# One-core graph-attention kernel: layer 1 gets three places for h and attention values two tiles behind, beside the transposes

## The reference, cut to what matters

```
# layer 0 of the reference (the layer that the title calls layer 1)
h = x @ W                                  # 12 heads of 64 features
th = tanh(h)
attn = (th @ w_src) + (th @ w_dst)^T       # per head, 64 x 64 per graph
attn = leaky_relu(attn, 0.2);  attn = where(adj, attn, -999);  attn = softmax(attn)
feat = elu(attn @ h + b)
gate = sigmoid(x @ H_w.T + H_b)
x = layernorm(x + gate * feat + (1 - gate) * x)
# second layer: six-head attention under the mask adj, output product, layernorm
```

## Time and profile before

| what | value |
|---|---|
| median of 3 runs | 2755.78 us (2752.92 to 2757.6) |
| the profiled execution's own time | 2753.85 us |
| its span | 2752.1 us |
| PE busy | 2723.5 us (99%) |
| PEld busy | 2516.5 us (91%) |
| DVE busy | 1679.9 us (61%) |
| ACT busy | 1211.6 us (44%) |
| POOL busy | 926.7 us (34%) |
| chain that ended last | PE 88%, DVE 6%, DMA 2%, issue 2%, ACT 1% |

### The profile page before, as it was taken

The page is one execution under the profiler, slowest core; times in us unless marked ns, Lnnn a source line. Parts: engine busy times, 40 slices in busy tenths (PEclk is TensorE's granted clock), DMA queues, the critical chain, the costliest instruction groups (busy, mean ns, idle before and its releaser), DMA issues.

```text
span 2752.1 us, 51889 instructions
## 1 busy us (share of the span) xinstructions
PE 2723.5 (99%) x20988; PEld 2516.5 (91%) x20988; DVE 1679.9 (61%) x3335; ACT 1211.6 (44%) x3109; POOL 926.7 (34%) x566
## 2 busy tenths in 40 slices
PE   8999999999999989999999999999999999999998
PEld 7777878888878889999999999999999999999998
DVE  7899998888888664444445444444545444444543
ACT  5666676666666633323332333323333333233332
POOL 2353334443444123323333233323332333323330
PEclk9999999999999999999999999999999999999999
DMA  6655665555555521222222222222222222222220
GB/s 183 172 138 145 168 161 135 145 138 141 143 137 138 169 75 58 82 70 81 59 69 71 82 70 58 81 79 73 59 71 72 79 70 63 77 82 70 59 70 24
DMA packets 306895, 269.50 MB, mean 98 GB/s; under 512 B 227808, under 2 KB 244192, under 8 KB 306656
## 3 DMA queue, kind: packets, MB, share of 16 engines
q1 hardware_dynamic: 306656, 266.19, 35.3%
HBM read 142.65 MB, written 75.89 MB: 79 GB/s over the span
## 4 chain that ended last, share of the span: by engine, by line
PE 88%; DVE 6%; DMA 2%; issue 2%; ACT 1%; POOL 0%; SPq 0%; DVEq 0%; ACTq 0%; POOLq 0%
PE ps_hg L1057 22%; PE ps_k L70 15%; PE ps_a L1232 15%; PE ps_a L70 14%; PE ps_q L70 14%; PE ps_s L1173 2%; PE ps_c L1198 2%; PE ps_pv L1089 1%; DMA dst_all<-dst_scratch 1%; PE ps_t L1076 1%; PE ps_pt L1198 1%; ACT logits L563 1%; DMA dst_scratch<-dst 1%; PE ps_pt L1180 1%; DVE logits L787 1%
## 5 line engine op out<-in xcount | busy, mean ns | idle before, releaser
L1057 PE MATMUL ps_hg<-w_hi,xT 128*128 128x512 f32 x2268 | 745.3, 401 | 3.0 <-DVE h_one L820 2.7
L1057 PEld LDWEIGHTS ps_hg<-w_hi,xT 128*128 128x128 f32 x2268 | 426.2, 188 | 106.2 <-issue 4.8
L1057 PE MATMUL ps_hg<-w_lo,xT 128*128 128x512 f32 x1134 | 448.5, 395 | 0.0
L70 PE MATMUL ps_k<-x1T_hi,wk_hi 128*128 128x256 f32 x1152 | 329.0, 286 | 0.0
L70 PE MATMUL ps_k<-x1T_lo,wk_hi 128*128 128x256 f32 x1152 | 321.8, 279 | 0.0
L70 PE MATMUL ps_k<-x1T_hi,wk_lo 128*128 128x256 f32 x1152 | 321.1, 279 | 0.0
L70 PE MATMUL ps_q<-x1T_hi,wq_hi 128*128 128x256 f32 x1140 | 319.3, 280 | 0.0
L70 PE MATMUL ps_q<-x1T_lo,wq_hi 128*128 128x256 f32 x1140 | 318.5, 279 | 0.0
L70 PE MATMUL ps_q<-x1T_hi,wq_lo 128*128 128x256 f32 x1140 | 317.8, 279 | 0.0
L653 ACT ACTIVATE qT<-ps_q,bq_col 128x256 f32<-128x256 f32 x192 | 80.7, 471 | 456.8 <-PE ps_q L70 456.7
L495 POOL TENSOR_TENSOR th_src<-th,wsrc_all 128x768 f32<-128x768 f32 x64 | 118.3, 1849 | 476.9 <-DVE dst_all L800 459.4
(11 more groups left out here) (156 smaller groups left out, 5755.3 us busy)
## 6 DMA issues: line engine op xcount, KB each, us to landing
x_tok<-x SPq DMA_DIRECT2D x64, 384.0 KB, 4.1
dst_all<-dst_scratch SPq DMA_DIRECT2D x128, 192.0 KB, 3.4
gate_scratch<-gate SPq DMA_DIRECT2D x64, 384.0 KB, 2.6
feat_scratch<-feat SPq DMA_DIRECT2D x128, 192.0 KB, 2.8
feat_in<-feat_scratch SPq DMA_DIRECT2D x62, 384.0 KB, 3.1
gate_in<-gate_scratch SPq DMA_DIRECT2D x62, 384.0 KB, 3.8
x_even<-x SPq DMA_DIRECT2D x16, 768.0 KB, 4.2
x_odd<-x SPq DMA_DIRECT2D x16, 768.0 KB, 4.4
```

The lines of the kernel that those rows point to most:

```text
L70: ins = pe.matmul(out, left[a][c], right[b][c], start=(n == 0), stop=(n == len(terms) - 1))
L1057: ins = pe.matmul(ps_hg[:, cols], left[a][c], right[b][c], start=(c == 0 and n == 0), stop=(c == KC - 1 and n == 2))
```

## The change

- `h_one` becomes a list of three places instead of two; `values(T-2)` moves on PE behind `project(2,T)`, next to `transpose_probs(T-1)`.
- `attention` and the ELU of a tile (`elu_exp`, `elu`, `store_feat`) run three tiles behind instead of two; the code after the loop changes with it.
- The product of tanh and w_src on POOL is written over tanh, and the place of `th_src` becomes the third place of h. `tanh_h` waits for the sum over that product.
- Masking and row maximum on DVE come in two pieces: the four heads that DVE made itself, then, behind the wait on Prelu, the eight heads of ACT.
- `spread_dst` reads back with one DMA instead of two and stands ahead of load_x and load_adj on SP.

```diff
             def spread_dst(T):
 ...
-                for g in range(2):
-                    sp.dma_start(dst_all[graph(g), :],
-                                 dst_rows[T % 2][g * D:(g + 1) * D].partition_broadcast(NODES)).then_inc(dst_in, 16)
+                both = dst_rows[T % 2].rearrange("(g f) -> g f", g=2).unsqueeze(1).to_broadcast([2, NODES, D])
+                sp.dma_start(dst_all[:, :], both).then_inc(dst_in, 16)
 ...
                 if TURNED <= T + 2 < NT:
                     turn_x(T + 2)
-                    if T + 3 < NT:
-                        load_x(T + 3)
+                spread_dst(T)
+                if TURNED <= T + 2 and T + 3 < NT:
+                    load_x(T + 3)
                 if T + 2 < NT:
                     sp.wait_ge(mask_done, T + 1)
                     load_adj(T + 2)
-                spread_dst(T)
 ...
-                if 2 <= T < NT - 1:
-                    store_feat(T - 2)
+                if 3 <= T < NT - 1:
+                    store_feat(T - 3)
 ...
+            sp.wait_ge(pv_done, NT - 2)
             feat_and_gate(1, 0)
             for n in range(EARLY_W1, 4 * KC):
                 load_chunk(sp, w1_chunks[n], w1_in[n])
+            store_feat(NT - 4)
             store_feat(NT - 3)
 ...                                                        # POOL
-                if T >= 1:
-                    pool.wait_ge(src_done, T)
-                pool.tensor_tensor(th_src[:, :], th[:, :], wsrc_all[:, :], ALU.mult).then_inc(thsrc_done, 1)
+                pool.tensor_tensor(th[:, :], th[:, :], wsrc_all[:, :], ALU.mult).then_inc(thsrc_done, 1)
 ...                                                        # ACT, tanh_h and the loop
-                    act.wait_ge(thsrc_done, T)
+                    act.wait_ge(src_done, T)
 ...
-                if T >= 2:
-                    elu_exp(T - 2)
+                if T >= 3:
+                    elu_exp(T - 3)
 ...                                                        # ACT, after the loop
             leaky_scores(NT - 1)
             copy_probs(NT - 2)
+            elu_exp(NT - 3)
             act.wait_ge(cols_in, 48)
             act.wait_ge(thsrc_done, NT)
             q_out(0, 0)
 ...                                                        # DVE
+            def masked_max(T, part, first, last):
+                n = last - first
+                scores_ = per_head(logits[:, first * NODES:last * NODES], n)
+                dve.copy_predicated(
+                    scores_, not_adj[:, T % 2, :].unsqueeze(1).to_broadcast([P, n, NODES]),
+                    masked[:, 0:1].unsqueeze(2).to_broadcast([P, n, NODES])).then_inc(masked_done, 1)
+                dve.wait_ge(masked_done, 2 * T + part + 1)
+                dve.tensor_reduce(neg_max[:, first:last], scores_, AX_X, ALU.max, negate=True).then_inc(max_done, 1)
 ...
-                dve.wait_ge(prelu_done, T + 1)
                 dve.wait_ge(leaky_done, T + 1)
                 dve.wait_ge(mask_done, T + 1)
-                dve.copy_predicated( ... all 12 heads ... )
-                dve.tensor_reduce( ... all 12 heads ... )
-                dve.wait_ge(max_done, T + 1)
+                masked_max(T, 0, ON_ACT, HEADS0)
+                dve.wait_ge(prelu_done, T + 1)
+                masked_max(T, 1, 0, ON_ACT)
+                dve.wait_ge(max_done, 2 * (T + 1))
 ...
                 dst_scores(T)
-                if T >= 2:
-                    attention(T - 2)
+                if T >= 3:
+                    attention(T - 3)
                 if T > 2:
                     bias_h(T)
 ...                                                        # DVE, after the loop
+            elu(NT - 4)
+            attention(NT - 3)
+            softmax_scores(NT - 1)
             elu(NT - 3)
-            softmax_scores(NT - 1)
             attention(NT - 2)
 ...                                                        # PE
                 project(1, T).then_inc(h_done, 1)
+                project(2, T).then_inc(g_done, 1)
                 if T >= 2:
                     values(T - 2)
-                project(2, T).then_inc(g_done, 1)
                 if T >= 2:
                     transpose_probs(T - 1)
```

More of the change, by code:

```diff
@@ L151, in two_graph_layers @@
         th = at(S + 21504, "th", [P, D])
[L152 to L155, removed]
+        h_hole = at(S + 24576, "h_hole", [P, HEADS0, EW])
+        Hb_less1 = at(S + 27712, "Hb_less1", [P, D])
+        dst_all = at(S + 30784, "dst_all", [P, D])
         th_dst = dst_all
-        logits = at(S + 33792, "logits", [P, D])
+        logits = at(S + 33856, "logits", [P, D])
         probs = logits
[L159 to L171, removed]
+        h_one = [at(S + 36928, "h_one0", [P, HEADS0, EW]), h_hole, at(S + 40064, "h_one2", [P, HEADS0, EW])]
+        probsT = at(S + 43200, "probsT", [P, HEADS0, NODES])
+        att = at(S + 46272, "att", [P, D])
+        ones = at(S + 46272, "ones", [P, P])
+        feat = at(S + 49344, "feat", [P, D])
+        gate = at(S + 52416, "gate", [P, D])
+        adj_u8 = at(S + 55488, "adj_u8", [P, 4, NODES], U8)
+        not_adj = at(S + 55744, "not_adj", [P, 2, NODES], U8)
+        dst = at(S + 55872, "dst", [P, HEADS0])
+        src = at(S + 55936, "src", [P, 2, HEADS0])
+        neg_max = at(S + 56032, "neg_max", [P, HEADS0])
+        row_inv = at(S + 56096, "row_inv", [P, 2, HB])
+        masked = at(S + 56160, "masked", [P, 1])
+        b_less1 = at(S + 56192, "b_less1", [P, E0])
         x1T_hi = at(S, "x1T_hi", [P, KC, GN], F32R)
@@ L556, in leaky_scores @@
             def leaky_scores(T):
-                act.wait_ge(dst_in, 32 * (T + 1))
+                act.wait_ge(dst_in, 16 * (T + 1))
                 act.wait_ge(src_done, T + 1)
@@ L584, in mask_of @@
                 if T >= 2:
-                    act.wait_ge(masked_done, T - 1)
+                    act.wait_ge(masked_done, 2 * (T - 1))
                 act.activation(not_adj[:, T % 2, :], adj_u8[:, T % 4, :], ACT.Copy, scale=-1.0, bias=1.0).then_inc(mask_done, 1)
@@ L770, in rest_x @@
                                       xT[:, T % 2, 0, :, :].bitcast(F32), ALU.subtract).then_inc(lo_done, 1)
+            def masked_max(T, part, first, last):
[6 more added lines that the diff above has]
+                dve.tensor_reduce(neg_max[:, first:last], scores_, AX_X, ALU.max, negate=True).then_inc(max_done, 1)
             def softmax_scores(T):
-                dve.wait_ge(dst_in, 32 * (T + 1))
+                dve.wait_ge(dst_in, 16 * (T + 1))
                 dve.wait_ge(src_done, T + 1)
@@ L817, in bias_h @@
                 dve.wait_ge(tanh_done, T + 1)
-                if T >= 2:
-                    dve.wait_ge(pv_done, T - 1)
-                dve.tensor_tensor(h_one[:, T % 2, :, 0:E0], per_head(ps_hg[:, 0:D], HEADS0),
+                if T >= 3:
+                    dve.wait_ge(pv_done, T - 2)
+                dve.tensor_tensor(h_one[T % 3][:, :, 0:E0], per_head(ps_hg[:, 0:D], HEADS0),
                                   b_less1[:, :].unsqueeze(1).to_broadcast([P, HEADS0, E0]),
@@ L825, in src_scores @@
                 dve.wait_ge(thsrc_done, T + 1)
-                dve.tensor_reduce(src[:, T % 2, :], per_head(th_src[:, :], HEADS0), AX_X, ALU.add).then_inc(src_done, 1)
+                dve.tensor_reduce(src[:, T % 2, :], per_head(th[:, :], HEADS0), AX_X, ALU.add).then_inc(src_done, 1)
             def bias_g(T):
@@ L885, in _ @@
             dve.memset(masked[:, :], MASKED0).then_inc(fixed, 1)
-            dve.memset(h_one[:, :, :, E0:EW], 1.0).then_inc(fixed, 1)
+            for place in h_one:
+                dve.memset(place[:, :, E0:EW], 1.0).then_inc(fixed, 1)
             rest_x(0)
@@ L890, in _ @@
             dve.wait_ge(memsets, 2)
-            dve.wait_ge(fixed, 2)
+            dve.wait_ge(fixed, 4)
             bias_h(0)
@@ L914, in _ @@
                 bias_g(T)
-                if T >= 2:
-                    elu(T - 2)
+                if T >= 3:
+                    elu(T - 3)
                 for t in range(GT):
@@ L1089, in values @@
                             ins = pe.matmul(ps_pv[graph(half), g, k * EW:(k + 1) * EW], probsT[graph(g), a, :],
-                                            h_one[graph(g), T % 2, a, :], start=True, stop=True)
+                                            h_one[T % 3][graph(g), a, :], start=True, stop=True)
                 ins.then_inc(pv_done, 1)
```

## The result

The changed kernel took 3073.09 us as the median of its runs (3072.22 to 3079.58), the kernel before 2755.64 us in the same comparison: a ratio of 1.1159, 95% interval [1.1143, 1.1176]. The forecast was 2764.0 us in a range of 2757 to 2770. The direction was right and the size was wrong by 309 us.

A forecast was written before the change was run, and what follows sets the result against it. It took PE to bound the kernel, with first-layer waits and the seam between layers. Order -2.5, waits -1.1 and seam +11.9 gave +8.3 us on 2753.85, so 2762.1, plus 1.9 to the median: 2764.0 us, range 2757 to 2770.

The forecast's parts named there:

- On the dst round trip: First layer, dst store and load: x load no longer ahead, one issue for two; gain 0 to 1.5 us a cycle, 0.5 taken.
- The waits of the first layer: PE's 5.1 us of waits in the first layer: 1.1 us taken back; bounds 5.1 won, 2 lost.
- up to 0.4 us a tile: First layer: what PE may lose when DVE's attention comes later than the 0.17 us cover before values.
- PE's order in the tile: Values beside the transposes on PE: gain 0.04 us a tile, 2.5 us over 62 tiles; bounds 0 and 5.6.
- The other waits of the first layer: First layer apart from the dst round trip: weight-rounding losses end, most early ones too, mixing tiles keep 0.3 us added DVE work.
- The stall in the tiles that round weights: First-layer tiles that round weights, a 14.77 us dst cycle: their loss was to end.
- The later x load: First layer: POOL's split of x starts some 2 us later, covered by POOL's idle time, at no cost.
- the margin of 0.17 us for attention: First layer: DVE's attention ends at 614.85, PE reaches values at 615.02, so an undisturbed tile loses nothing.
- attention too late for values: Rival: PE meets the new wait by 0.1 us in each first-layer tile, 6 us more, 2770 us; chance 0.13.
- The seam: Between the layers: ACT's elu_exp waits for tile 60's late store, PE stalls 15.5 us; net cost 11.9 us, bounds 7.5 to 14.2.
- the first old stall: PE's 5.51 us wait for wv_lo in group 0 behind the first layer: to be swallowed, with its 2.3 us at half clock.
- Sum: Whole kernel: -2.5 - 1.1 + 11.9 = +8.3 us, a forecast median of 2764.0 us; this case had chance 0.72.

The follow-up runs named there:

- e1: The changed kernel with its single spreading load of dst put back to two loads of 64 rows: 2769.69 us, ratio 1.0053.
- e2: The kernel before with only the single spreading load of dst from the change: 3114.43 us, ratio 1.1304.
- e5: e3 with the x load put back ahead of spread_dst on SP: 2758.2 us, ratio 1.0011.
- e6: e3 with attention(T-2) at the end of DVE's tile instead of attention(T-3) ahead of bias_h: 2755.57 us, ratio 1.0002.
- e7: e3 with both the x load ahead of spread_dst and attention at the end of DVE's tile: 2754.49 us, ratio 0.9995.
- e9: e7 with elu(NT-4) ahead of rest_x1(0) on DVE and store_feat(NT-4) ahead of SP's waits after the loop: 2750.03 us, ratio 0.9981.
- e3: e1 with the feature store of tile NT-4 issued ahead of the 12 weight chunks instead of behind them: 2761.21 us, ratio 1.0025.
- e4: The changed kernel with two dst loads of 64 rows, source written 4 x 16 x 768: 2928.2 us.
- e8: The changed kernel with two dst loads of 64 rows, source written 8 x 8 x 768: 2798.6 us.

## Why the prediction was wrong, point by point

- **The step that failed: "On the dst round trip ... one issue replaces two: 0 to 1.5 us"** of gain, inside "The waits of the first layer". I counted the issue that the merged load saves and put its own length at no change, without a reason: I took for granted that it would run as the two halves had. It runs on two DMA engines and takes 10.3 us instead of 3.7. The shape in the diff, 2 x 64 x 768, showed it. The range had no bound for this, and the "up to 0.4 us a tile" for a late DVE became 210.4 us in 61 waits, 3.4 each. e1 and e2 show that this term alone is 303 to 360 us.
- **PE's order in the tile: right.** Forecast 0.04 us a tile, from 14.313 to 14.27. Measured 14.26 to 14.27 in nearly all tiles without a wait of e1, e5, e6, e7 and e9. Its timeline in e1 answers to the earlier trace rows:

```profile
600.99 0.40 PE L1065 MATMUL ps_hg<-w_hi,xT 128*128 128x512 f32 x1
601.32 0.93 PE L1097 MATMUL ps_pv<-h_one,probsT 64*64 64x65 f32 x48
602.18 0.88 PE L1084 MATMUL ps_t<-ident,logits 128*128 128x128 f32 x6
602.81 0.48 PE L1065 MATMUL ps_hg<-w_hi,xT 128*128 128x512 f32 x1
```

  The gaps are 0.33, 0.86 and 0.63, as summed. By the rule in the Trainium skill, "TensorEngine Tiling (Array Packing)", Key Properties, that a change of tiling mode drains TensorE, the prediction had set a gain of 0 against this; the measured 0.05 us a tile speaks for the sum.
- **The other waits of the first layer: wrong in size.** I took back 1.1 of the 5.1 us; in e1 they grew instead. Its 61 tiles take 878.6 us where 61 x 14.27 is 870.5, so the waits are 8.1 us, and what PE's order gained was lost again. The stall in the tiles that round weights was to end and became 0.45 us in each of eight tiles (ten in e3). The later x load was priced at nothing: POOL's idle time hid the split on POOL, but not what the split does to DVE beside it. And the margin of 0.17 us for attention was too thin there. That rival, "attention too late for values", came true in 13 places with 7.4 us in e1, not in every tile.
- **The seam: mechanism right, size near.** ACT was to stand some 15 us in elu_exp for the store of tile 60, PE 15.5 us ahead of the transposes of tile 63, the first old stall to vanish, the second to grow to 4.3 us. Measured in e1: 14.1, 14.5, none, and 4.4. The stretch behind the last mark grew by 14.8 us (2766.3 - 930.25 against 1821.2); the sum took 11.9 and named 14.2 as its bound if the second stall cost clock again. It did, 0.50 from 1002.7 to 1009.5 around a wait of 4.4 us, and 14.8 is 0.6 us above that bound. In the changed kernel itself ACT waits 11.1 us there and PE 13.6.
- **Sum.** Without the slow load the forecast of 2764.0 stands against e1's 2769.7. By the profiled executions it had 2.9 us too little for the seam, 4.0 too little for the loop (878.6 against 874.6), and 1.0 too much ahead of the loop's first mark (51.67 against 52.65). The 303 us above that come from one edit. By the seam alone the direction would have come out right too, but nearly all of the measured loss has another cause, which the prediction did not hold.

## What to carry to other kernels

Before merging two DMAs into one, look at the slowest dimension of the new pattern: a leading 2 left all but two of the sixteen DMA engines idle here (busy share 0.13), and the load went from 3.7 to 10.3 us at the same bytes. When work goes one tile further back in a pipeline, follow it to the code behind the loop, where its wait can end up ahead of everything else on its engine. And a transfer that moves by 5 us moves what it releases: look at what will then run beside it on another engine.

## What the runs showed of the hardware that was not expected

- DMA time at equal bytes went 10.6, 7.8, 5.6 and 3.6 to 5.0 us for 2, 4, 8 and 64 or more entries in the slowest dimension, beside the x load and the features behind it. It does not halve at each step.
- A load on few engines delays what is queued behind it: the x load, written over 128 rows, landed after 10.9 us behind the changed kernel's load, 7.9 behind e4's, 5.7 behind e8's and 4.4 behind e1's. In e2, where it is issued ahead of the slow load, it took 4.0.
- A POOL copy of 16-bit planes that began 0.17 us before a DVE step over two SBUF operands stretched that step from 0.42 to 1.57 us; it ended 0.27 us after the copy.
